# Edge tables with a partition's four rows side by side, and index copies one group ahead, in a four-layer graph network kernel

## What is computed

```
L0: three times  h = act(h @ W_self.T + b + mean over edges into dst of h[src] @ W_neigh.T)
L1: ho = mean over edges into dst of (h[src] - edge_attr);  hi = mean over edges out of src of (h[dst] - edge_attr)
    h = (ho @ W_O.T + b_O + hi @ W_I.T + b_I + h @ W_S.T + b_S) / 3, then batch norm over all nodes
L2: messages h[src] @ W_msg.T + b_msg + embed[edge_type], summed into dst, then a GRU cell for every node
L3: y = h @ W.T + b;  mean over edges out of src of y[dst], 0 where a node has none
x = x + layer(relu(layernorm(x)))
```

## Time and profile before

| | |
|---|---|
| median of 3 runs | 7188.97 us (7172.65 to 7218.53) |
| the profiled execution's own time | 7174.61 us, its span 7172.9 us |
| PE busy | 4872.3 us, 68% |
| DVE busy | 4001.9 us, 56% |
| ACT busy | 2896.9 us, 40% |
| POOL busy | 4067.1 us, 57% |
| DMA | 1152936 packets, 1139.31 MB, mean 159 GB/s |
| packets under 2 KB | 989377 |

### The profile page before, as it was taken

The page is one execution under the profiler, slowest core; times in us unless marked ns, Lnnn a source line. Parts: engine busy times, 40 slices in busy tenths (PEclk is TensorE's granted clock), DMA queues, the critical chain, the costliest instruction groups (busy, mean ns, idle before and its releaser), DMA issues. The chain is left out here.

```text
span 7172.9 us, 109212 instructions
## 1 busy us (share of the span) xinstructions
PE 4872.3 (68%) x23937; PEld 3547.8 (49%) x23937; DVE 4001.9 (56%) x14866; ACT 2896.9 (40%) x6394; POOL 4067.1 (57%) x4659
## 2 busy tenths in 40 slices
PE   4676745558787787633646537799999978844553
PEld 2454533335565566623643325576666644434553
DVE  5665646654564566733323215667999989943210
ACT  0465634433563464323001100346888855533000
POOL 0655556640550354666556650576888877765555
PEclk9898866679999998855778867558999989955766
DMA  2344446659678767944546537444445445434443
GB/s 85 119 154 135 142 142 188 191 167 327 218 224 272 247 222 222 287 141 135 166 133 138 104 52 226 131 129 141 171 171 171 171 136 146 120 108 123 80 69 47
DMA packets 1152936, 1139.31 MB, mean 159 GB/s; under 512 B 109586, under 2 KB 989377, under 8 KB 1152421
## 3 DMA queue, kind: packets, MB, share of 16 engines
q1 hardware_dynamic: 1011970, 962.41, 42.5%
q0 software_dynamic: 140800, 175.08, 11.7%
HBM read 703.03 MB, written 456.06 MB: 162 GB/s over the span
## 5 line engine op out<-in xcount | busy, mean ns | idle before, releaser
L1061 POOL DMA_INDIRECT G_x<-node_table,G_idx x400 | 397.9, 995 | 165.6 <-issue 135.6
L1061 POOL DMA_INDIRECT G_V<-layer_rows,G_idx x400 | 382.1, 955 | 165.4 <-issue 97.3
L1914 PE MATMUL bank<-O_r,O_eq 125*125 125x128 f32 x1600 | 286.4, 362 | 239.3 <-ACT O_out L1940 207.3
L1073 POOL DMA_INDIRECT out<-O_out,O_idx x200 | 315.2, 1576 | 212.2 <-DMA out<-O_out,O_idx 150.9
L1091 PE MATMUL bank<-first_last_indicators,G_V 125*128 (+1 forms) x1600 | 282.1, 298 | 223.6 <-DVE G_V L1740 132.4
L1073 POOL DMA_INDIRECT node_table<-H_out,H_idx x200 | 318.8, 1594 | 171.1 <-DMA node_table<-H_out,H_idx 116.2
L1420 PE MATMUL bank<-B_S,B_V 127*128 127x125 f32 x2000 | 313.4, 302 | 147.0 <-DVE B_S L1408 109.8
L1914 PEld LDWEIGHTS bank<-O_r,O_eq 125*125 125x125 f32 x1600 | 279.0, 275 | 246.7 <-issue 163.7
L1091 PEld LDWEIGHTS bank<-first_last_indicators,G_V 125*128 125x128 f32 x1600 | 276.2, 260 | 233.7 <-issue 179.5
L1058 POOL COPY G_idx<-i_tb 128x4 int32 (+1 forms) x100 | 19.1, 191 | 613.2 <-POOLq L255 497.2
L1420 PEld LDWEIGHTS bank<-B_S,B_V 127*128 127x128 f32 x2000 | 274.8, 211 | 180.4 <-issue 108.2
(11 more groups left out here) (472 smaller groups left out, 15867.2 us busy)
## 6 DMA issues: line engine op xcount, KB each, us to landing
P_x<-node_table SPq DMA_DIRECT2D x196, 512.0 KB
B_V<-values SPq DMA_DIRECT2D x250, 256.0 KB
B_krow<-keys_dst SPq DMA_DIRECT2D x250, 250.0 KB
values<-G_V SPq DMA_DIRECT2D x200, 256.0 KB
BN_g<-node_table SPq DMA_DIRECT2D x195, 256.0 KB
out<-P_out SPq DMA_DIRECT2D x195, 256.0 KB
node_table<-G_xg SPq DMA_DIRECT2D x97, 512.0 KB
layer_rows<-A_a SPq DMA_DIRECT2D x100, 256.0 KB
```

Of the source, the lines that this page charges most:

```text
L1061: pool.indirect_dma_start(out=rows[u % len(rows)][:, c, :], out_offset=None, in_=table, in_offset=bass.IndirectOffsetOnAxis(ap=idx[u % len ...
L1073: pool.indirect_dma_start(out=table, out_offset=bass.IndirectOffsetOnAxis(ap=idx[u][:, c:c + 1], axis=0), in_=rows[u][:, c, :], in_offset= ...
L1914: last = nc.tensor.matmul(m.bank[2 + u % 2][0:EP, d * D:(d + 1) * D], eq[u][:, c, d * EP:(d + 1) * EP], r[u][:, c, :], start=(c == 0), sto ...
```

## The change

1. **Layout.** `edge_rows` and `value_tiles` map rows as `(p c)`: partition p holds rows 4p to 4p+3 of its group, 2 KB in one piece. The numbers of rows that are computed on the chip (`posf`, `epos`) follow. `share_segments` writes each of its four tiles by four transfers of 25 rows in place of one of 100, since its rows now lie in another stride. `attr_rows` (the edges' own features, 512-byte pieces) and the batch norm's loads stay as they are.
2. **Index copies.** In every gather or scatter loop POOL copies the indices of group i + 1 before it issues the transfers of group i (new helper `next_index`), and its wait for group i's copy refers to one made a group earlier. Before it reuses an index tile it waits until the gather or scatter of four groups before has landed.
3. In B5 POOL's loop is unrolled by 4 instead of 8.

```diff
 def edge_rows(table, i):
-    return table[bass.ds(i * ROWS, ROWS), :].rearrange("(c p) f -> p c f", p=128)
+    return table[bass.ds(i * ROWS, ROWS), :].rearrange("(p c) f -> p c f", c=TILE)
...
-            nc.gpsimd.iota(posf[:], [[128, T]], base=0, channel_multiplier=1, allow_small_or_imprecise_dtypes=True).then_inc(s_p, 1)
+            nc.gpsimd.iota(posf[:], [[ROWS, T // TILE], [1, TILE]], base=0, channel_multiplier=TILE, allow_small_or_imprecise_dtypes=True).then_inc(s_p, 1)
...
+def next_index(nc, f, index, idx, s_idx, g, w, landed=None):
+
+    if f.has(g):
+        if landed:
+            f.landed(landed, g - 4, w % 4, 64)
+        nc.gpsimd.tensor_copy(idx[w % 4][:], index[:, bass.ds(g * TILE, TILE)]).then_inc(s_idx, 1)
+
+
+def gather(nc, pool, f, idx, s_idx, i, u, table, rows, landed):
+
     f.after(s_idx, i)
     for c in range(TILE):
...
-                        sp.dma_start(table[c * TC:(c + 1) * TC, EP + k, :], R[k][c][:]).then_inc(s_out, 16)
-                sp.wait_ge(s_out, 64)
+                        for q in range(TILE):
+                            sp.dma_start(table[EP + k, c * TC // TILE:(c + 1) * TC // TILE, q, :], R[k][c][q:TC:TILE, :]).then_inc(s_out, 16)
+                sp.wait_ge(s_out, 64 * TILE)
...
-                    f.after(s_h, i - 4)
-                    f.landed(s_xo, i - 4, u)
-                    gather(nc, pool, f, m.i_src, idx_s, s_is, i, u, a["x"], xs_whole, s_gs)
-                    gather(nc, pool, f, m.i_dst, idx_d, s_id, i, u, a["x"], xd_whole, s_gd)
+                    next_index(nc, f, m.i_src, idx_s, s_is, i + 1, u + 1, s_gs)
+                    next_index(nc, f, m.i_dst, idx_d, s_id, i + 1, u + 1, s_gd)
+                    if has(i):
+                        f.after(s_h, i - 4)
+                        f.landed(s_xo, i - 4, u)
+                        gather(nc, pool, f, idx_s, s_is, i, u, a["x"], xs_whole, s_gs)
+                        gather(nc, pool, f, idx_d, s_id, i, u, a["x"], xd_whole, s_gd)
...
-                    f.after(s_o, i)
-                    f.landed(s_sc, i - 4, u, 64)
-                    scatter(nc, pool, f, index, idx, s_i, i, u, table, out_whole, s_sc, add=True)
-
-                sweep(pool, 0, n, n - 1, body, back=4, ahead=0, special=0)
+                    next_index(nc, f, index, idx, s_i, i + 1, u + 1, s_sc)
+                    if has(i):
+                        f.after(s_o, i)
+                        scatter(nc, pool, f, idx, s_i, i, u, table, out_whole, s_sc, add=True)
+
+                sweep(pool, -1, n, n - 1, body, back=4, ahead=1, special=0)
```

More of the change, by code:

```diff
@@ L1053, in edges_setup, with scatter @@
     keep.close()
-def gather(nc, pool, f, index, idx, s_idx, i, u, table, rows, landed):
-    nc.gpsimd.tensor_copy(idx[u % len(idx)][:], index[:, bass.ds(i * TILE, TILE)]).then_inc(s_idx, 1)
+def next_index(nc, f, index, idx, s_idx, g, w, landed=None):
[4 more added lines that the diff above has]
+def gather(nc, pool, f, idx, s_idx, i, u, table, rows, landed):
     f.after(s_idx, i)
     for c in range(TILE):
[L1061 to L1068, removed]
+        pool.indirect_dma_start(out=rows[u][:, c, :], out_offset=None, in_=table,
+                                in_offset=bass.IndirectOffsetOnAxis(ap=idx[u][:, c:c + 1], axis=0)).then_inc(landed[u], 16)
+def scatter(nc, pool, f, idx, s_idx, i, u, table, rows, landed, add=False):
     f.after(s_idx, i)
     if add:
-        f.landed(landed, i - 1, u - 1, 64)
+        f.landed(landed, i - 1, (u - 1) % 4, 64)
     for c in range(TILE):
@@ L1524, in body @@
                 f = Flow(pool, has, m)
[L1525 to L1529, removed]
+                next_index(nc, f, m.i_tb, idx, s_i, i + 1, u + 1, s_g)
+                if has(i):
+                    f.landed(s_vo, i - 4, u)
+                    f.after(s_hl, i - 4)
+                    gather(nc, pool, f, idx, s_i, i, u, table, V_whole, s_g)
+            return -1, n, n - 1, 0, body
         def sync(sp):
@@ L1700, in body @@
                     f = Flow(pool, has, m)
-                    f.after(s_h, i - 4)
-                    gather(nc, pool, f, m.i_src2, idx, s_i, i, u, m.XH, x_whole, s_g)
-                sweep(pool, 0, n, n - 1, body, back=4, ahead=0, special=0)
+                    next_index(nc, f, m.i_src2, idx, s_i, i + 1, u + 1, s_g)
+                    if has(i):
+                        f.after(s_h, i - 4)
+                        gather(nc, pool, f, idx, s_i, i, u, m.XH, x_whole, s_g)
+                sweep(pool, -1, n, n - 1, body, back=4, ahead=1, special=0)
             @block.sync
@@ L1794, in body @@
                     f = Flow(pool, has, m)
-                    f.after(s_g, i)
-                    f.landed(s_sc, i - 4, u, 64)
-                    scatter(nc, pool, f, m.i_dst2f1, idx, s_i, i, u, m.XH, g_whole, s_sc)
-                sweep(pool, 0, n, n - 1, body, back=4, ahead=0, special=0)
+                    next_index(nc, f, m.i_dst2f1, idx, s_i, i + 1, u + 1, s_sc)
+                    if has(i):
+                        f.after(s_g, i)
+                        scatter(nc, pool, f, idx, s_i, i, u, m.XH, g_whole, s_sc)
+                sweep(pool, -1, n, n - 1, body, back=4, ahead=1, special=0)
                 finish(pool, s_sc, n, 64)
@@ L2056, in body @@
                     f = Flow(pool, has, m)
-                    f.after(s_x2, i - 4)
-                    gather(nc, pool, f, m.i_src, idx, s_i, i, u, m.XG, x_whole, s_g)
-                sweep(pool, 0, n, n - 1, body, back=4, ahead=0, special=0)
+                    next_index(nc, f, m.i_src, idx, s_i, i + 1, u + 1, s_g)
+                    if has(i):
+                        f.after(s_x2, i - 4)
+                        gather(nc, pool, f, idx, s_i, i, u, m.XG, x_whole, s_g)
+                sweep(pool, -1, n, n - 1, body, back=4, ahead=1, special=0)
             @block.sync
@@ L2218, in body @@
                         nc.gpsimd.tensor_tensor(dT[v % 2][:], hT[v][:], nT[v][:], ALU.subtract).then_inc(s["d"], 1)
+                    g = Flow(pool, has, m)
+                    next_index(nc, g, m.i_dst, idx, s_i, i + 3, u + 3, s_x)
                     if has(i + 2):
[L2220 removed]
                         g.after(s["x2"], i - 2)
[L2222 to L2224 removed]
+                        gather(nc, pool, g, idx, s_i, i + 2, (u + 2) % 4, m.XG, x_whole, s_x)
+                sweep(pool, -3, n, n + 4, body, back=7, ahead=3, special=0)
             @block.vector
@@ L2563, in body @@
                     f = Flow(pool, has, m)
-                    f.landed(s_x, i, u)
-                    scatter(nc, pool, f, m.i_dstf, idx, s_i, i, u, m.out, x_whole, s_sc)
-                sweep(pool, 0, n, n - 1, body, back=4, ahead=0, special=0)
+                    next_index(nc, f, m.i_dstf, idx, s_i, i + 1, u + 1, s_sc)
+                    if has(i):
+                        f.landed(s_x, i, u)
+                        scatter(nc, pool, f, idx, s_i, i, u, m.out, x_whole, s_sc)
+                sweep(pool, -1, n, n - 1, body, back=4, ahead=1, special=0)
                 finish(pool, s_sc, n, 64)
```

39 lines of the change are left out of this document (19 added, 20 removed).

## The result

The changed kernel is slower: 7518.9 us (median of 4 runs, 7515.5 to 7541.8) against 7187.3 us for the kernel before in the same comparison (4 runs, 7172.7 to 7218.5), ratio 1.046, interval 1.044 to 1.049. The forecast was 7005 us, and none of its rivals names the mechanism. The loss isn't tied to the code alone: in other comparisons the kernel before itself took 6856 us, and there the copies ahead alone made it 4.2% faster. Most of what follows is about that difference.

The account below looks back on a forecast made before the run. It took DMA to bound B1, POOL's uncounted issue gaps many stages, and PE, DVE or scatter landing others. Savings of 22+38+60+25+15+28 less 13 gave 175 us off 7174.6, so 7000, put at 7005 us; range 6945 to 7090.

Parts of the forecast that it names:

- POOL's gap: In gather and scatter loops: the 0.81 us between index copy and first transfer falls to 0.27 to 0.30 us.
- G1, G2, lookup and positions: Stages where POOL is ahead of the dense work: closing its gap gains nothing unless that work becomes quicker.
- B4 and O1: Scatter stages: shorter gap before each group's first scatter saves 30 us each, 60 together.
- A ... I take 38: Stage A, two index copies per group: 38 us saved, bounds 20 and 43, since POOL already waits for ACT.
- B5: Stage B5: shorter gap before the gathers saves 15 us, bounds 0 and 22, since DVE is busy.
- Wait for landing of group i-3: POOL's new wait before reusing an index tile: taken to cost nothing.
- Layout: B1 and B2: 2 KB pieces at 95 ns replace four of 512 B, saving 28 us together, bounds 0 and 40.
- Rival 3: Larger DMA pieces bring nothing: 28 us and some of B3's gain lost, 7035 us; chance 8%.
- Shared steps: `share_segments`, five times: sixteen write issues instead of four cost 13 us in all, bounds 3 and 43.
- Rival 4: H and O2: scatters land later behind SP's larger pieces, +54 us, 7059 us; chance 9%.
- 5: G4 gets the full PE clock: some 40 us more off, 6965 us; chance 8%.
- Rival 6: G1 and G2 lose PE clock: 7383 us at 0.50, deciding below 0.68; chance 4%.

Follow-up runs that it names:

- 14: Changed kernel with four writes per shared step and POOL again waiting for the copy just issued, against the kernel before (7177 us): 7208 us, ratio 1.004.
- 13: The changed kernel, unchanged, timed again against the kernel before (7177 us): 7500 us, ratio 1.045.
- experiment 2: Only the index copies ahead, with old layout and old shared step, against the kernel before: 6563 us, ratio 0.958.
- experiment 1: Only the new layout with sixteen writes per shared step, old index copies, against the kernel before (6856 us): 6852 us, ratio 1.000.
- experiment 3: Index copies a group ahead, but POOL waits for the copy just issued before its transfers, against the kernel before: 6847 us, ratio 0.998.
- 9: Changed kernel with four writes per shared step and POOL again waiting for the copy just issued, against the kernel before (6846 us): 6796 us, ratio 0.993.
- experiment 4: Only the new layout, with four writes of 100 rows per shared step instead of sixteen of 25, against the kernel before: 6809 us, ratio 0.994.

## Why the prediction was wrong

- **Failed step: the sum takes POOL's gap as pure loss.** "G1, G2, lookup and positions: POOL is ahead of the dense work; nothing", "B4 and O1 ... 60 together", "A ... I take 38". In the late condition the gap was also what kept signals of PE, and in G3 of DVE, from coming later still. Without it: positions +124, O1 +58 for -30, A +132 for -38, B3 +28 for -25, G4 +17 for 0, B4 +9 for -30, G3 +10 for -22. That the missing gap does it is shown by putting it back (14 against 13, in one comparison: positions -105, O1 -62, B3 -31, G4 -22 us) and by the table of lateness; in A one break per eight transfers won back only 37 us, two in another comparison 118. Lookup's +18 is not the break's: with it back the stage takes 396 us, and what makes it stays open. No rival had a mechanism in which a quicker POOL slows another engine without sharing its data.
- **The gap's size was right,** and a little better than thought: 0.17 us behind the copy where 0.27 and 0.30 were assumed. In the prompt condition, where nothing else happens, the terms can be read (experiment 2 against 1, which has the layout): G3 -22 (forecast -22), B4 and O1 -74 (-60), B3 -28 (-25), A -59 (-38), B5 -33 (-15), and positions, lookup, G1 and G2 -35, -25, -11, -9 (0). A and the four others were under-sized: POOL was the limit in stages that I had put down to PE and DVE from a late trace. Lateness had lengthened them to 364 us in G1 where 297 is enough, 380 in lookup for 292, 658 in A for 628. B5 takes 479 us in both conditions, and why it gives more than its bound of 22 stays open.
- **What was luck.** G3, O1 and B4 were forecast at 282, 284 and 294 us and took 281, 277 and 287 in the prompt condition; but I had read them from a late trace without knowing it. They hold because these three stages of the kernel before take the same time in both (305 and 303, 314 and 314, 324 and 324).
- **Wait for landing of group i-3: nothing,** as forecast; it is in experiments 3, 9 and 14 as well, and experiment 3 takes 6847 us where the layout alone takes 6852.
- **Layout: right sign, size off.** B1 and B2 -48 for -28 (bound 40). Packet time is share times length: 1.00 x 205 us before, 0.96 x 182 after, 30 us less per stage where I had 14. A piece of 2048 B takes 85.5 ns in B1, four of 512 B took 110, which is 20 us; the other 11 come from the pieces of 2000 B beside them, 86 ns each for 96. The 95 ns read from P were too high because two thirds of P's bytes go in pieces of 4096 B, 200 ns each, while its pieces of 2048 B take 84. Rival 3 falls: pieces over 512 B did bring time. That rival went by the smallest piece at line rate in the Trainium skill, "DMA: Bandwidth & Descriptors", Specifications; the traces differ from it, with 512 B in 27.5 ns and 2048 B in 85.5.
- **Shared steps: +45 for +13,** just over the bound 43. 16 issues took 11.72 us, 0.73 each. I had put 0.34 on an issue because one of 100 rows took 0.30; but that one had the old address pattern, and in the new one 100 rows take 0.75 (experiment 4). Together with B1 and B2 the layout came to nothing (experiment 1).
- **H, O2, P and BN** were as forecast, within 5 us. In H and O2 POOL waits some 2 to 4 us per group for a landing, so it has a break anyway.
- **Rival 4, 5 and 6** didn't happen: O2 566, G4's clock 0.50, G1's 0.96. Rival 6's price at a clock of 0.68 doesn't follow from its own numbers: 405 us of PE in stages of 364 are 41 us each, 82 together and not 240. PE's clock did fall where nobody had looked, in the scatters of positions, 0.88 to 0.59.

**What stays open.** What makes a comparison late or prompt. Whether PE's results are late besides its signals. How POOL's issuing reaches the others' signals, and whether it is the idle time in the break that helps or the lower rate of transfers: all breaks tested in the late condition were of one kind. Why four transfers with a break of 0.8 us are harmless in O1 and B4 but leave 2 us of lateness per group in G1 and G2, and lookup at 380 us for 292. And the changed kernel as it is was never timed in the prompt condition; from experiments 1 and 2 (6563, and nothing for the layout) I estimate near 6560 us.

## What to carry to other kernels

A gap on one engine can be what another lives on: before closing it, look for waits whose releaser, by the profile, is a transfer of a stage long over, and ask what was really waited for. Time a change of 4% in more than one comparison if the kernel before can differ by 5% between them; this one was +4.6% or, in its main part, -4.2%, by a condition that no line of code shows, though one row of the trace does: SP's longest MOVE. And price a DMA issue from a row with the same address pattern, times the issues that follow each other without a wait.

## What the runs showed of the hardware

- In the late condition some of SP's own register instructions take 0.7 us. The same instruction of O1, shortest, median and longest in ns, in the changed kernel (late; 12 of the 36 take 0.69 to 0.71 us) and in the copies ahead alone (prompt). The kernel before, late, has 29/29/29 in O1, where nothing is late in it, but 17 of 145 stretched ones in G1 and 45 of 253 in A:

```profile
L2599 SPq MOVE O_x<-x_of_dst x36: 7/29/711, 6650.2 to 6905.3; - x36
```

```profile
L2598 SPq MOVE O_x<-x_of_dst x36: 29/29/29, 5769.7 to 5950.8; - x36
```

- A write occupied SP for 0.69 us with 25 rows in the new layout (median of 16 in the step after A), for 0.74 with 100 rows in the new layout (median of 4, experiment 4) and for 0.30 with 100 rows in the old.
- In the late condition the update of a semaphore of VectorE can stand in the trace 4.3 us after the step that makes it has ended (3498.43 and 3502.69 in G3 above).
- Executions without a profile took the same time as those with one (7515.5 to 7541.8 us, span 7517.8), so the lateness is not the profiler's.
